# One stage of a fused two-layer kernel: order of GpSimd's low parts, and how ternary weights are formed

## The reference, cut to what matters

```python
x = x + _L0_ffn_ref(_L0_cond2_ref(x, Wg, Wu, Wd, Ag, Bg, Au, Bu, Ad, Bd, adapter), w1, w3, w2)

def _L0_cond2_ref(...):                      # 256 -> 1024 -> 256, rank-16 adapters chosen per sequence
    gate = x @ Wg + (x @ A_g[i]) @ B_g[i]
    up   = x @ Wu + (x @ A_u[i]) @ B_u[i]
    h    = silu(gate) * up
    return h @ Wd + (h @ A_d[i]) @ B_d[i]

def ternary_quant(w):                        # _L0_ffn_ref: 256 -> 682 -> 256, with this on w1, w3, w2
    s = mean(abs(w))
    return clip(round(w / s), -1, 1) * s
g = silu(x @ w1q.T) * (x @ w3q.T)
return g @ w2q.T
```

## Time and profile before

| what | value |
|---|---|
| median of 3 runs | 1397.94 us (1395.5 to 1398.98) |
| the profiled execution, its own time | 1397.21 us |
| its span, first to last instruction | 1395.4 us |
| PE busy | 1307.0 us, 94% of the span |
| DVE, POOL, ACT busy | 930.4, 567.4, 518.5 us |
| mean granted TensorE clock | 0.978 |

### The profile page before, as it was taken

How to read it: one execution, slowest core, us unless ns; L and a number is a source line. 1 busy time by engine, 2 the same in 40 slices (tenths; PEclk the granted TensorE clock), 3 DMA queues, 4 the chain that set the end, 5 groups by cost and what they waited for, 6 DMA issues and landing times. The chain is left out here.

```text
span 1395.4 us, 36886 instructions
## 1 busy us (share of the span) xinstructions
PE 1307.0 (94%) x14806; PEld 1055.5 (76%) x14806; DVE 930.4 (67%) x1822; ACT 518.5 (37%) x1202; POOL 567.4 (41%) x624
## 2 busy tenths in 40 slices
PE   4999999999999999999999989999997789997997
PEld 3788888888888888888878868788775567775665
DVE  3888778887888787788786673343423346666886
ACT  3344444444444444444454222222322223222442
POOL 1756655556665566655565222221312111112111
PEclk9999999999999999999999999999998889997998
DMA  6000000000000000000011120000001700001610
GB/s 201 6 13 13 13 13 14 19 25 13 13 13 13 28 13 13 13 16 22 13 43 58 61 62 1 0 1 0 0 0 65 223 23 0 0 0 40 193 50 23
DMA packets 35536, 46.47 MB, mean 33 GB/s; under 512 B 7214, under 2 KB 24840, under 8 KB 35272
## 3 DMA queue, kind: packets, MB, share of 16 engines
q1 hardware_dynamic: 33048, 43.81, 10.4%
q10 hardware_dynamic: 2272, 0.52, 0.2%
q0 software_dynamic: 80, 0.26, 0.1%
HBM read 42.22 MB, written 2.36 MB: 32 GB/s over the span
## 5 line engine op out<-in xcount | busy, mean ns | idle before, releaser
L448 PE MATMUL OE<-w_o,ogT_s 128*128 128x256 f32 x512 | 137.7, 392 | 0.0
L907 POOL TENSOR_TENSOR hs_lo<-work,hs_hi 128x512 fp32r<-128x512 f32 x44 | 57.9, 1317 | 178.4 <-ACT hs_hi L1209 178.4
L250 POOL TENSOR_TENSOR turned<-raw 128x512 f32<-128x512 f32 x62 | 78.8, 1272 | 121.5 <-DVE raw L683 121.5
L708 DVE RECIPROCAL enz<-SC 128x128 f32<-128x128 f32 x128 | 121.1, 947 | 2.0 <-PE SC L396 1.9
L291 POOL TENSOR_TENSOR exz<-ex,enz 128x256 f32<-128x256 f32 x64 | 47.5, 742 | 132.4 <-ACT ex L611 132.4
L339 PE MATMUL PJ<-hs_hi,w_hi 128*128 128x512 f32 x248 | 101.3, 408 | 0.0
L350 PE MATMUL PJ<-w_hi,hs_hi 128*128 128x512 f32 x256 | 100.6, 393 | 0.0
L350 PE MATMUL PJ<-w_lo,hs_hi 128*128 128x512 f32 x256 | 100.1, 391 | 0.0
L350 PE MATMUL PJ<-w_hi,hs_lo 128*128 128x512 f32 x256 | 99.8, 390 | 0.0
L339 PE MATMUL PJ<-hs_lo,w_hi 128*128 128x512 f32 x248 | 97.2, 392 | 0.0
L339 PE MATMUL PJ<-hs_hi,w_lo 128*128 128x512 f32 x248 | 96.9, 391 | 0.0
(11 more groups left out here) (409 smaller groups left out, 3477.5 us busy)
## 6 DMA issues: line engine op xcount, KB each, us to landing
we_ring<-in_we SPq DMA_DIRECT2D x64, 256.0 KB, 3.1
w_raw<-in_w_slices SPq DMA_DIRECT2D x64, 128.0 KB, 2.5
xres<-in_x SPq DMA_DIRECT2D x2, 1024.0 KB, 8.3
turned<-in_w_slices SPq DMA_DIRECT2D x4, 512.0 KB, 4.4
w_o<-in_wo SPq DMA_DIRECT2D x4, 512.0 KB, 5.2
out_rows<-xres SPq DMA_DIRECT2D x16, 128.0 KB, 1.7
w1r<-in_w1i SPq DMA_DIRECT2D x1, 1408.0 KB, 6.5
raw<-in_w SPq DMA_DIRECT2D x2, 682.0 KB
```

What stands on the lines that cost most here:

```text
L250: pool.tensor_tensor(to[:, 0, :], x1c[:, :], x2s[:, :], ALU.subtract)
L448: m = pe.matmul(OE[:, SW:SW + D], ogT_s[:, i % 2, h * P:(h + 1) * P], w_o[i // G % 2][:, h, :], start=(h == 0), stop=(h == HQ - 1))
L708: dve.reciprocal(enz[:, cols], SC[:, SW:2 * SW][:, cols]).then_inc(z_rec, 1)
L907: eng.tensor_tensor(hT[1][s, m % 2, :], h[s, m % 2, :], hT[0][s, m % 2, :].bitcast(F32), ALU.subtract).then_inc(second, 1)
```

## The change

Three edits, all in `mlp0`:

- POOL's order in the second half of a step becomes: low part of block 0, of `ugm`, of block 1, of `uum`, of block 2, of block 3. In the early part (attention step 59) the two low parts stay next to each other.
- `u_first` and `u_second` count each tile alone: ACT makes the high part of `ugm` on its own signal (`ug_mask`), POOL waits for each high part, and PE waits for twice the count.
- `ternary` has three passes and no mask: scale and bound by 1 from above; bound by -1 from below and add `RND` (12582912.0, at which f32 holds whole numbers only, so the sum is rounded); take `RND` away and write the result. `link` stands behind the first and the second.

```diff
--- before.py
+++ after.py
@@ -942,10 +942,9 @@
             cols = slice(n * F, (n + 1) * F)
             pool.tensor_tensor(w[1][:, 1, cols], b_raw[:, cols], w[0][:, 1, cols].bitcast(F32), ALU.subtract).then_inc(b_second, 1)
 
-        def u_low(i):
-            pool.wait_ge(u_first, i + 1)
-            pool.tensor_tensor(u_p[0][1], ugm, u_p[0][0].bitcast(F32), ALU.subtract)
-            pool.tensor_tensor(u_p[1][1], uum, u_p[1][0].bitcast(F32), ALU.subtract).then_inc(u_second, 1)
+        def u_low(i, n):
+            pool.wait_ge(u_first, i * 2 + n + 1)
+            pool.tensor_tensor(u_p[n][1], (ugm, uum)[n], u_p[n][0].bitcast(F32), ALU.subtract).then_inc(u_second, 1)
 
         def early(i):
             n = i - STEPS
@@ -953,7 +952,8 @@
                 b_low(0)
             if n == -5:
                 b_low(1)
-                u_low(0)
+                u_low(0, 0)
+                u_low(0, 1)
             if n in (-4, -3):
                 h_low(pool, n + 5, n + 4, slice(0, P), h_first, h_second)
             if n == -2:
@@ -964,10 +964,10 @@
         def step(i, nxt=True, start=0):
             for m in range(start, FC - 1):
                 h_low(pool, i * FC + m + 1, m, slice(0, P), h_first, h_second)
-            if nxt:
-                u_low(i + 1)
             for m in range(HC - 2):
                 h_low(pool, i * HC + m + 1, m, slice(0, hw[m]), f_first, f_second)
+                if nxt and m < 2:
+                    u_low(i + 1, m)
 
         def main():
             step(0, start=2)
@@ -1035,7 +1035,7 @@
                 gate_part(0, part, 0)
                 if part == 1:
                     pe.wait_ge(b_second, 2)
-                    pe.wait_ge(u_second, 1)
+                    pe.wait_ge(u_second, 2)
                     bias_part(0, 0, 0)
                     bias_part(0, 1, 0)
             elif n in (-3, -2):
@@ -1065,7 +1065,7 @@
 
         def gates(i, m):
             if m == 0:
-                pe.wait_ge(u_second, i + 1)
+                pe.wait_ge(u_second, i * 2 + 2)
             if m >= 2:
                 pe.wait_ge(h_mul, i * FC + m - 1)
             else:
@@ -1192,9 +1192,9 @@
             act.activation(w[0][:, 1, 2 * F:2 * F + FC * D], wd_raw, ACT.Copy).then_inc(wd_first, 1)
 
         def u_high(i):
-            act.wait_ge(u_mask, i + 1)
-            act.activation(u_p[0][0], ugm, ACT.Copy)
-            act.activation(u_p[1][0], uum, ACT.Copy).then_inc(u_first, 1)
+            for n, ready in enumerate((ug_mask, u_mask)):
+                act.wait_ge(ready, i + 1)
+                act.activation(u_p[n][0], (ugm, uum)[n], ACT.Copy).then_inc(u_first, 1)
 
         def gate_tanh(i, m, e):
             act.wait_ge(gate_mm, i * FC + m + 1)
@@ -1359,10 +1359,9 @@
 
         def ternary(to, x, col, p=P):
 
-            link(dve.tensor_scalar(x, x, scl[0:p, col:col + 1], None, ALU.mult))
-            dve.tensor_scalar(to, x, 0.5, None, ALU.is_gt)
-            link(dve.tensor_scalar(x, x, -0.5, None, ALU.is_lt))
-            return dve.tensor_tensor(to, to.bitcast(F32), x, ALU.subtract)
+            link(dve.tensor_scalar(x, x, scl[0:p, col:col + 1], 1.0, ALU.mult, ALU.min))
+            link(dve.tensor_scalar(x, x, -1.0, RND, ALU.max, ALU.add))
+            return dve.tensor_scalar(to, x, -RND, None, ALU.add)
 
         def sizes():
             dve.wait_ge(tern_in, 64)
```

## The result

The changed kernel takes 1389.82 us in the median of 13 runs (1386.75 to 1394.72), beside 1398.30 us of the kernel before (13 runs, 1395.5 to 1402.34). The ratio on record is 0.9944, with a 95% interval of 0.9930 to 0.9958: 0.56% faster, 7.8 us (the two medians alone differ by 8.5 us). Its profiled execution took 1389.55 us, its span is 1387.7 us.

The account below looks back on a forecast made before the run. PE was taken to bound the kernel up to layer 0's end, so only removing its stops gains. 2.38 + 1.64 + 3.57 = 7.59 us off the profiled 1397.21, set midway toward the median: 1390.0 us, range 1387.0 to 1394.0.

Parts of the forecast that it names:

- Part 1: Step 0, ternary passes: rank result 2.38 us earlier, 0.63 from block 7's low part starting earlier and 1.75 from `t2`.
- Part 2: Step 0, behind the rank-product stop: with 1.5 us of stop left PE's clock stays at 2.4 GHz, gaining 1.64 us.
- the rival: Clock behind step 0's rank-product stop falls all the same, or the fall was one run's: gain 5.95 us; chance 0.19.
- Part 3: Second half of steps 0 to 2: POOL's new order removes PE's stop ahead of the first `fdown`, 3.57 us in all.
- Passed on whole behind layer 0: After the barrier behind layer 0 nothing is late from before, so the whole 7.59 us reaches the program's end.
- a new wait: Second half: another wait takes the place of POOL's stop ahead of `fdown`; gain 4.0 us, 1393.6 us; chance 0.10.
- slow passes: Ternary on DVE: two-operation passes run at the two-tensor pace; gain 3.8 us, 1393.8 us; chance 0.06.
- a lasting low clock: Clock stays low through step 0's second half, costing nearly 20 us more: slower, 1412 us; chance 0.03.
- the fourth: Rival that the low clock lasts through step 0's second half, making the kernel slower, 1412 us; chance 0.03.

Follow-up runs that it names:

- t2_only: Kernel before, with three ternary passes for the third matrix only and four for the first two; 1393.96 us beside 1397.85, ratio 0.9964.
- pair_behind_0: Changed kernel, but POOL takes both rank low parts right behind block 0 and block 1's only after both; 1393.81 us beside 1397.85, ratio 0.9959.
- again: The changed kernel run once more, with no further edit, beside the second group's runs; 1390.26 us beside 1396.87, ratio 0.9947.
- t2_early: Changed kernel, with the big piece of the third matrix formed ahead of block 7's low part; 1388.64 us beside 1396.87, ratio 0.9938.
- tern_only: Kernel before, with the three-pass ternary alone, POOL's order and the counts as they were; 1394.30 us beside 1397.85, ratio 0.9974.

## Why the prediction was right

Forecast 1390.0 us, range 1387.0 to 1394.0, measured 1389.82. Its steps:

- **Part 1, 2.38 us: right, in both terms.** The stretch got 2.38 us shorter. The moved start of block 7's low part gave 0.65 (0.63 forecast) and `t2` 1.73 (1.75), told apart by t2_only. A pass with two operations costs what one with one does: 0.88 us at 1280 elements in both kernels. The stop left is 1.52 us (1.5 forecast).
- **Part 2, 1.64 us: right, and the runs tie it to the length of the stop.** Behind stops of 1.50 to 1.70 us the clock stayed at 1.00 in each of the five executions with one. Behind 3.41, 3.42, 3.15 and 4.72 us it fell in each of the four. That is one profiled execution for each kernel, two for the changed one. The transposes ahead of the stop, on which the rival rested, did not matter at 1.5 us. The way to it was weaker than I wrote: that the stop of 2.50 us in step 3 was followed by 1.00 was luck of that execution (last section), and the prediction leaned on it.
- **Part 3, 3.57 us: right in mechanism, a little small.** The three stretches gave 3.48 us, and another 0.28 us came behind `fdown`. No other wait took its place: block 1's low part was done at 830.37 + 1.30 = 831.67 and PE took it up at 832.08, 0.4 us of slack where 0.5 was forecast. That slack was all the prediction said for taking the tiles in turn; pair_behind_0 shows that both right behind block 0 are too much for it. Places further back in POOL's queue were not run.
- **Passed on whole behind layer 0: not shown to the tenth.** Layer 1 took 327.6 us in place of 327.2; in the ten executions that I have it took 325.0 to 330.1 us, in no order with the edits. The sum of 7.59 us stands against 8.08 in layer 0 and 7.7 in the spans.
- **The rivals.** Neither a new wait, nor slow passes, nor a lasting low clock came. Against the fourth the prediction said that the clock was back within 4 us of PE's return; that was misread. PE returned at 821.84 and was at full pace only at 826.77, 4.9 us later (rows in the first section). The rival fell because the clock stayed up, not by that argument. The median's gain of 8.5 us (7.8 by the ratio) is within what such shifts make.

What the 0.28 us is: PE in step 1, the last matmul ahead of `fdown`, its first, and the first of block 3. After:

```profile
900.89 0.39 PE L1148 MATMUL PJ<-zT_lo,tern 128*128 128x512 f32 x1
901.12 0.28 PE L1097 MATMUL AW_TA<-tern,hs_hi 128*128 128x256 f32 x1
...
902.06 0.40 PE L1148 MATMUL AW_TA<-zT_hi,tern 128*128 128x512 f32 x1
```

Before, the last two of these:

```profile
907.58 0.39 PE L1097 MATMUL AW_TA<-tern,hs_hi 128*128 128x256 f32 x1 [1.03 <-POOL hs_lo L907]
...
908.62 0.39 PE L1148 MATMUL AW_TA<-zT_hi,tern 128*128 128x512 f32 x1
```

The eight matmuls of `fdown` took 902.06 - 901.12 = 0.94 us after and 908.62 - 907.58 = 1.04 us before. The first matmul behind a stop takes one full spacing more; I had counted the stop to its end and not that. That is 0.1 us in each step.

## What to carry to other kernels

Where PE is the bound, list its stops and ask of each which engine's queue held the operation that ended it: here POOL worked until 833.17 on two tiles that PE wanted only in the next gated stage (its first matmul is at 843.83), while PE stood for a third, and the order of three lines was worth as much as a faster arithmetic. A pass saved on an engine that nobody waits for can still count, if it lets the next thing on that engine start as early as its own inputs allow. Count a stop of PE by the distance of starts and together with what the clock does behind it, and settle gains of 0.1 to 0.3% by marks in the trace, since the whole program's time spreads by more.

## What the runs showed of the hardware

**The clock behind a stop of 2.50 us goes either way.** The stop in step 3 is the same in all ten executions. In four of them the second half took 5.7 us from its first matmul to its first `fdown`, in six 7.0 to 7.2 us. The changed kernel was profiled twice and shows both: 5.7 us in the first execution, and in "again" the second kind, with the window behind it (granted clock 0.60):

```profile
1041.57 0.50 PE L1149 MATMUL PJ<-zT_hi,tern 128*128 128x512 f32 x1 [2.50 <-DVE zT_lo L1419]
```

```profile
1043.00:1047.00 4.00, 4.00 (x13) 3.12 (x12) 1.55 (x3) 1.82 (x3) 1.10 (x1) 0.60 0.01 4
```

The execution of before happened to be of the first kind. In all ten another stop, of 0.8 us, lies 1.7 us of PE's work ahead of this one, which none of the shorter stops of step 0 had so close; what it adds was not tested. There are other falls in the rest of that half, so the two kinds differ by less in the end: it took 20.7 to 21.7 us in all. The Trainium skill, TensorE: Matmul & The Clock Gate, in its part on the HAM clock gate, says that the watching isn't tied to the program, so that the point of a change differs between runs. The two executions of the changed kernel agree with that. The count over these stops is: behind 1.50 to 1.70 us a fall in none of five, behind 2.50 us in six of ten, behind 3.15 to 4.72 us in each of four.

**A pass over a ternary matrix on DVE and a low part on POOL exclude each other, and the order of arrival decides.** A third pass of a ternary matrix took 1.84 us where it came behind POOL's start (1.82 in t2_early), and 0.83 to 0.87 us alone; POOL's took 1.30 us when it came first (t2_early) and 1.76 when a two-tensor pass of DVE was running. Not every operation of DVE does it: in the kernel before, the two passes of gated block 7 (L1320 at 811.86, L1326 at 812.57) fall in or across POOL's 1.76 us (811.32 to 813.08) and took their usual 0.68 and 0.69 us. The Trainium skill, SBUF — State Buffer, section Who interferes with whom, calls that an exclusive lock on a shared pair of ports, held for the whole instruction; the numbers agree.

**The start of a program varies.** The mark at the sums of absolute values lies at 792.1 to 793.2 us in six executions and at 795.0 to 795.4 us in four, in no order with the edits, which all lie behind it or change nothing ahead of it that PE waits for. The changed kernel shows both starts (792.66 and, in "again", 795.16). Together with the 5 us of spread behind layer 0 it fits that single runs of one kernel lie 8 us apart and more (9.5 in tern_only), though only one or two executions of a kernel have a trace. What makes the two starts stays open.
